# Routing of a mixture of experts in batches of two and four groups, one batch ahead of the shared expert

## The reference

```python
xf = layernorm(x).reshape(-1, 128)
shared = einsum(silu(xf @ sw1) * (xf @ sw3), sw2)      # 256 hidden
logits = xf @ router_w.T + experts_bias                # 8 experts
rw, sel = top_k(logits, 2)
rw = softmax(rw)
moe = sum over the two chosen experts of rw * (silu(xf @ w1[e]) * (xf @ w3[e])) @ w2[e]
x = x + moe + shared
```

## Time and profile before

| | us |
|---|---|
| median of 3 timed runs (lowest, highest) | 1047.42 (1047.19, 1048.82) |
| the profiled execution: its span, which is all that it has as a time of its own | 1165.9 |
| stage of the gates and the mLSTM | 0 to 216 |
| shared part with the routing | 216 to 451.6 |
| routed part | 451.6 to 624 |
| attention | 624 to 1024 |
| per-expert FFN | 1024 to 1166 |

### The profile page before, as it was taken

How to read it: one execution, slowest core, us unless ns; L and a number is a source line. 1 busy time by engine, 2 the same in 40 slices (tenths; PEclk the granted TensorE clock), 3 DMA queues, 4 the chain that set the end, 5 groups by cost and what they waited for, 6 DMA issues and landing times. The chain is left out here.

```text
span 1165.9 us, 24805 instructions
## 1 busy us (share of the span) xinstructions
PE 969.0 (83%) x9121; PEld 680.7 (58%) x9121; DVE 734.8 (63%) x2271; ACT 535.2 (46%) x848; POOL 505.3 (43%) x566
## 2 busy tenths in 40 slices
PE   6819998667787749999994478888888899989998
PEld 1217776444444426666662267777777778856665
DVE  7676999765566545877774555554555556445553
ACT  2457886432333325666665134453444446332221
POOL 4202675676566652555555773344533531011110
PEclk9869998677879768999998578888888989999999
DMA  8554553321222235333332111101110210024331
GB/s 258 192 148 138 159 165 106 128 89 51 57 61 66 61 89 149 109 124 123 119 119 82 46 33 33 29 28 38 44 31 29 83 49 21 21 65 111 93 93 36
DMA packets 84600, 101.29 MB, mean 87 GB/s; under 512 B 36129, under 2 KB 57313, under 8 KB 83713
## 3 DMA queue, kind: packets, MB, share of 16 engines
q1 hardware_dynamic: 73552, 81.61, 23.5%
q0 software_dynamic: 8192, 16.79, 4.7%
q10 hardware_dynamic: 2736, 1.31, 0.4%
HBM read 64.81 MB, written 30.67 MB: 82 GB/s over the span
## 5 line engine op out<-in xcount | busy, mean ns | idle before, releaser
L1728 ACT ACTIVATE split_table<-attn_psT 128x1024 f32<-128x1024 f32 x64 | 65.5, 1023 | 170.0 <-DMA early_ctxT<-in_ctxT 95.9
L1039 POOL TENSOR_TENSOR moe_h_lo<-moe_hid,moe_h_hi 128x512 f16<-128x512 f32 x78 | 90.3, 1158 | 100.2 <-ACT moe_h_hi L1196 95.4
L1619 PE MATMUL attn_psO<-heads_vheads,split_table 128*64 128x18 f32 x2048 | 87.2, 220 | 30.1 <-issue 30.0
L1302 DVE SCALAR_TENSOR_TENSOR moe_hid<-moe_psU,split_to_hidden,moe_act_g 128x512 f32<-128x512 f32 x110 | 81.0, 748 | 36.5 <-ACT moe_act_g L1190 36.4
L1190 ACT ACTIVATE moe_act_g<-moe_psG,split_unscale 128x512 f32<-128x512 f32 x110 | 75.7, 688 | 59.7 <-PE moe_psU L1121 38.6
L1619 PEld LDWEIGHTS attn_psO<-heads_vheads,split_table 128*64 128x64 f32 x2048 | 78.3, 148 | 41.6 <-issue 39.7
L1791 DVE TENSOR_REDUCE split_table<-attn_psN 128x16 f32<-128x1024 f32 x62 | 75.8, 1222 | 22.4 <-DMA early_ctxT<-in_ctxT 9.6
L1815 DVE RECIPROCAL split_table<-attn_psO 128x16 f32<-128x16 f32 x64 | 16.5, 257 | 112.7 <-PE attn_psO L1619 50.8
L1033 POOL DMA_INDIRECT scratch_xs<-cell_xn,res_row x64 | 63.3, 989 | 42.4 <-DVE res_row L1296 25.2
L1196 ACT ACTIVATE moe_h_hi<-moe_hid 128x512 f16<-128x512 f32 x110 | 68.5, 623 | 24.3 <-DVE moe_hid L1302 23.3
L1033 POOL DMA_INDIRECT scratch_xs<-moe_xn,res_row x64 | 62.6, 978 | 37.2 <-DVE res_row L1296 19.4
(11 more groups left out here) (282 smaller groups left out, 2762.9 us busy)
## 6 DMA issues: line engine op xcount, KB each, us to landing
early_ctxT<-in_keys SPq DMA_DIRECT2D x16, 512.0 KB, 3.5
scratch_ys<-cell_h SPq DMA_DIRECT2D x26, 256.0 KB, 2.0
early_ctxT<-in_values SPq DMA_DIRECT2D x8, 544.0 KB, 3.5
mlstm_vals<-in_values SPq DMA_DIRECT2D x8, 544.0 KB, 3.5
res_x<-in_x SPq DMA_DIRECT2D x16, 256.0 KB, 6.2
early_ctxT<-in_ctxT SPq DMA_DIRECT2D x16, 256.0 KB, 6.5
attn_in_ctxT<-attn_in_ctxT SPq DMA_DIRECT2D x64, 64.0 KB
scratch_x<-split_table SPq DMA_DIRECT2D x16, 256.0 KB
```

The costliest lines, as they stand in the source:

```text
L1039: pool.tensor_tensor(h_lo[u % 3][c][:, :], hid[u % 2][c][:, :], h_hi[u % 3][c][:, :], ALU.subtract).then_inc(lo_done[c], 1)
L1302: v.scalar_tensor_tensor(out=hid[u % 2][c][:, :], in0=psU[c][:, :], scalar=sw.to_hidden[:, 0:1], in1=act_g[c][:, :], op0=ALU.mult, op1=ALU ...
L1619: ins = pe.matmul(psO[i % 2][b2 * S:(b2 + 1) * S, at * 2 * VW1:(at + 1) * 2 * VW1], probT[i % 2][:, rr, b2, mp, n * S:(n + 1) * S], vheads ...
L1728: act.activation(probT[i % 2][:, :, :, :, :].rearrange("p r b m q -> p (r b m q)"), psT[:, :], ACT.Exp).then_inc(prob_done, 1)
```

## The change

Routing is done in batches of groups, (0,1), (2,3), (4 to 7), (8 to 11), (12 to 15), one batch ahead of the shared expert. A group that is routed gets transposes of its own (`turn_route`, copied by ACT in `route_out`), apart from those of the shared expert, through the same bank `psT`. In iterations g with g % 4 of 0 or 1 and g < 12 two groups of the next batch are normalised, transposed and routed. For a whole batch there is one pass of logits and choice (`read_logits`, `settle`; maxima and indices still go by tiles), at g % 4 = 2, one `tensor_tensor_scan` for the sums over tiles, two count matmuls, and one `place_`, at g % 4 = 3; the running sum enters as the first element of the scan, so `carry` goes. Batches 0 and 1 are routed ahead of the loop, except for count and placing of batch 1, which come in iteration 0. The normalised groups have eight buffers, four of them views of the weight buffers of the routed part, whose first copies therefore wait for scatters and transposes. The slot map is made at g = 12 instead of after the loop, and the tails are cleared from there; K and V are projected two groups behind, in pairs for the last four, so none is left after the loop.

POOL's order is as before. The core of the diff:

```diff
+BATCHES = ((0, 2), (2, 2), (4, 4), (8, 4), (12, 4))
+BATCH_OF = [k for k, (_, n) in enumerate(BATCHES) for _ in range(n)]
+BATCH_TILES = max(n for _, n in BATCHES) * TILES
...
+        held = [wt[k][:, :, :].rearrange("p w h -> p (w h)").bitcast(F32)[:, 0:GROUP].rearrange("p (t d) -> p t d", t=TILES) for k in range(NW)]
+        xb = [xn[0], xn[1], held[0], held[1], xn[2], xn[3], held[2], held[3]]
...
+        def routed_at(g):
+            first = (g // 4 + 1) * 4 + g % 4 * 2
+            return (first, first + 1) if g % 4 < 2 and first < GROUPS else ()
+
+        def projected_at(g):
+            if g < BEHIND:
+                return ()
+            return (g - BEHIND,) if g < GROUPS - BEHIND else (GROUPS - 4 + 2 * (g - GROUPS + BEHIND), GROUPS - 3 + 2 * (g - GROUPS + BEHIND))
...
-            for g in range(GROUPS - AHEAD):
+            for g in range(GROUPS - LAST_MOVES):
                 move_values(sp, g)
-            sp.wait_ge(tails_done, ONE + 1)
-            for e in range(E0 - ACT_TAILS):
-                clear_tail(sp, e)
+                if g == GROUPS - 6:
+                    sp.wait_ge(tails_done, ONE + 1)
+                    for e in range(E0 - ACT_TAILS):
+                        clear_tail(sp, e)
...
-                pool.wait_ge(placed, ONE + g + 1)
+                pool.wait_ge(placed, ONE + BATCH_OF[g] + 1)
...
+            def turn_route(n):
+                pe.wait_ge(xn_done, ONE + max(n - 1, 0))
+                pe.wait_ge(x_lo_done, ONE + reads["shared"])
+                pe.wait_ge(xnT_done, ONE + n)
                 for t in range(TILES):
-                    ins = pe.matmul(psR[:, t * E0:(t + 1) * E0], xnT[g % 2][:, t * P:(t + 1) * P], router[:, :], start=True, stop=True)
+                    ins = pe.transpose(psT[:, t * P:(t + 1) * P], xb[n % XN][:, t, :], ident[:, :])
+                ins.then_inc(route_turned, 1)
+                reads["routed"] = n + 1
...
+            def count_(k):
+                n = BATCHES[k][1] * TILES
+                pe.wait_ge(either_done, ONE + k + 1)
+                pe.wait_ge(placed, ONE + k)
+                if k == len(BATCHES) - 1:
+                    pe.matmul(psC, every[:, :], sums_of[n][:, :, n], start=True, stop=True)
+                pe.matmul(psK[:, 0:E0 * n], earlier[:, :], chain_of[n][:, :, 1:n + 1], start=True, stop=False)
+                pe.matmul(psK[:, 0:E0 * n], every[:, :], sums_of[n][:, :, 0:n], start=False, stop=True).then_inc(counted, 1)
...
+            turn_route(0)
+            turn_route(1)
+            route(0)
+            route(1)
+            turn_route(2)
+            turn_route(3)
+            route(2)
+            route(3)
+            count_(0)
             turn(0)
...
+                if g == 0:
+                    count_(1)
+                if new:
+                    turn_route(new[0])
+                if g == BEHIND:
                     pe.wait_ge(given.loaded, ONE + 16 * given.count)
-                if g >= AHEAD:
-                    project_k(g - AHEAD)
+                behind = projected_at(g)
...
+                if new:
+                    route(new[0])
+                    turn_route(new[1])
                 if g >= 2:
                     down(g - 2)
-                count_(g)
-                if g >= AHEAD:
-                    project_v(g - AHEAD)
-            total()
-            for g in range(GROUPS - AHEAD, GROUPS - 1):
-                project_k(g)
-                if g == GROUPS - 2:
-                    down(g)
-                project_v(g)
+                if new:
+                    route(new[1])
+                if behind:
+                    project_v(behind[0])
+                if g % 4 == 2 and g < GROUPS - 4:
...
+            def read_logits(k):
+                first, groups = BATCHES[k]
+                n = groups * TILES
+                v.wait_ge(routed, ONE + first + groups)
+                v.tensor_tensor(logits[:, 0:n, :], psR[:, 0:E0 * n].rearrange("p (t e) -> p t e", e=E0),
+                                bias[:, :].unsqueeze(1).to_broadcast([P, n, E0]), ALU.add).then_inc(logits_read, 1)
+                v.wait_ge(logits_read, ONE + k + 1)
+                for t in range(n):
...
+            def settle(k):
+                first, groups = BATCHES[k]
+                n, cols = groups * TILES, slice(first * TILES, (first + groups) * TILES)
+                step(v.tensor_copy(wheref[:, 0:n, :], where[:, 0:n, 0:2]))
+                step(v.tensor_tensor(chosen[:, cols, :, :], wheref[:, 0:n, :].unsqueeze(3).to_broadcast([P, n, 2, E0]),
+                                     iota[:, :].unsqueeze(1).unsqueeze(1).to_broadcast([P, n, 2, E0]), ALU.is_equal))
+                if k:
+                    v.wait_ge(counted, ONE + k)
+                    was = BATCHES[k - 1][1] * TILES
+                    v.tensor_copy(chain_of[n][:, :, 0], sums_of[was][:, :, was])
+                else:
+                    v.memset(chain_of[n][:, :, 0], 0.0)
+                step(v.tensor_tensor(chain_of[n][:, :, 1:n + 1].rearrange("p e t -> p t e"), chosen[:, cols, 0, :], chosen[:, cols, 1, :], ALU.add))
+                v.tensor_tensor_scan(sums[:, 0:E0 * (n + 1)], keeps[n][:, :, :].rearrange("p e t -> p (e t)"), chains[:, 0:E0 * (n + 1)],
+                                     0.0, ALU.mult, ALU.add).then_inc(either_done, 1)
+                v.wait_ge(either_done, ONE + k + 1)
...
+                if j < NW:
+                    n = XN + (2, 3, 6, 7)[j]
+                    v.wait_ge(scattered[n % XN], 16 * 2 * TILES * (GROUPS // XN))
+                    v.wait_ge(turned, ONE + n + 1)
...
+            normalise(2)
+            normalise(3)
             cell.next_statistics(v, GROUPS - 3)
+            v.wait_ge(front.loaded, ONE + 16 * len(front.consts))
+            read_logits(0)
+            settle(0)
+            place_(0)
             low_x(0)
-            v.wait_ge(front.loaded, ONE + 16 * len(front.consts))
-            choose(0)
+            read_logits(1)
+            settle(1)
...
+                for n in routed_at(g):
+                    normalise(n)
                 gated(g, 0)
                 gated(g, 1)
+                if g == 0:
+                    place_(1)
                 if g < 2:
                     cell.next_statistics(v, GROUPS - 2 + g)
-                if g + 2 < GROUPS:
-                    normalise(g + 2)
-                place_(g)
-                ins = carry(g)
-                if g + 1 < GROUPS:
-                    step(ins)
-                    choose(g + 1)
-                else:
-                    ins.then_inc(either_done, 1)
+                if g % 4 == 3 and g < GROUPS - 4:
+                    place_(g // 4 + 2)
+                if g % 4 == 2 and g < GROUPS - 4:
+                    read_logits(g // 4 + 2)
+                    settle(g // 4 + 2)
                 low_part(g)
                 if g >= 2:
                     add(g - 2)
-            map_tiles()
+                if g == GROUPS - 4:
+                    map_tiles()
```

More of the change, by code:

```diff
@@ L941, in phase_moe @@
         hid = [[r.sb(f"hid{u}{c}", [P, GROUP]) for c in range(CH0)] for u in range(2)]
-        past, past_tiles = (hid[0][c][:, 0:SLOT_TILES * E0].rearrange("p (j e) -> p j e", e=E0) for c in range(2))
-        full = past_tiles[:, 0:GROUPS, :].rearrange("p g e -> p e g")
         h_hi = [[r.sb(f"h_hi{u}{c}", [P, GROUP], F16) for c in range(CH0)] for u in range(3)]
@@ L1014, in _ @@
                 load(j)
-            for g in range(GROUPS - AHEAD, GROUPS - 1):
+            for g in range(GROUPS - LAST_MOVES, GROUPS - 1):
                 move_values(sp, g)
@@ L1054, in _ @@
         def _(pe):
+            reads = {"shared": 0, "routed": 0}
             def turn(u):
@@ L1178, in xT_out @@
                 act.wait_ge(turned, ONE + u + 1)
-                if u < GROUPS:
-                    if u >= 2:
-                        act.wait_ge(routed, ONE + u - 1)
-                    act.activation(xnT[u % 2][:, :], psT[:, :], ACT.Copy)
                 if u >= 2:
@@ L1185, in xT_out, with route_out @@
                 act.activation(x_hi[u % 2][:, :], psT[:, :], ACT.Copy, scale=X_SCALE).then_inc(x_hi_done, 1)
+            def route_out(n):
+                act.wait_ge(route_turned, ONE + n + 1)
+                if n >= 2:
+                    act.wait_ge(routed, ONE + n - 1)
+                act.activation(xnT[n % 2][:, :], psT[:, :], ACT.Copy).then_inc(xnT_done, 1)
             def gate(u, c):
@@ L1215, in _ @@
                     high_part(u - 1, 1)
+                if new:
+                    route_out(new[0])
                 gate(u, 1)
                 high_part(u, 0)
-                if u >= AHEAD:
-                    k_out(u - AHEAD)
-            v_out(GROUPS - 1 - AHEAD)
-            high_part(GROUPS - 1, 1)
-            for g in range(GROUPS - AHEAD, GROUPS - 1):
-                k_out(g)
-                v_out(g)
-                if g == GROUPS - AHEAD:
+                if behind:
```

(37 more changed lines are left out.)

129 lines of the change are left out of this document (58 added, 71 removed).

## The result

The changed kernel takes 1073.61 us in the median of four runs (1068.45 to 1086.33), the kernel before 1047.31 in the same comparison. The ratio is 1.0225 with a 95% interval of 1.0183 to 1.0267: 24 us slower, between 19 and 28 (the run at 1086.33, which had the lowest mean clock, is left out of it). The prediction said 1070 and slower.

A forecast was written before the change was run, and what follows sets the result against it. It took POOL's chain of scatters, 10.1 us a group, to bound the shared stage, the other engines' loop close behind. Timed 1047.4 + 10.5 (late startup and loop) + 12 (clock) = 1070 us, range 1036 to 1090.

The forecast's parts named there:

- The reading of the first profile: Shared stage and attention: the profile's waits are not in timed runs; scatters end at 396, routed stage begins about 404.
- The missing 118 us: Profiled span over timed median: 71 us in attention groups under the gathers plus 47 us ahead of the routed stage.
- The 4.87 us between the count and the addition: Group 14, 405.71 to 410.58: could be real PE work recorded too early, since matmul ends in a profile are estimates.
- POOL's second step: Root and scatter(1) wait for statistics(15): scatter(1) at 253 to 257, POOL idle 9 to 13 us more.
- The loop: PE, ACT and DVE in the shared stage: iterations of 12.3, 12.2 and 8.2 us, 143 us from low_x(2).
- The clock: PE idle about 3.2 us in eight iterations drops to half clock: 2.8 us each, 0 to 22, taken as 12.
- One sign of the list: Profile of the changed kernel: granted clock below 0.8 in the shared stage.
- K and V ahead of the routed part: Last four groups' K and V leave the time after the loop: gives 0 to 2 us.
- Eight buffers: Normalised groups, eight buffers instead of four: remove waits not seen in the profile, 0 us.
- The scan: Running sum on DVE: between 0.2 and 0.7 us per batch, 0.3 taken; five make 1 us either way.
- That the stalls are real: Rival, faster: late count releases also in timed runs, POOL's 44.5 us of waiting go; 1002 to 1022; chance 0.20 with milder form.
- POOL bound on both sides: Rival, same: statistics(15) ready before 241, iterations under 10.1 us, scatters end as now, 1047 us; chance 0.07.

The follow-up runs named there:

- the second profile: The kernel before, unchanged, profiled once more: 1047.91 us, span 1046.1.
- the clock held up: Changed kernel with unused matmuls on PE in its idle time ahead of routing transposes and batch counts: 1069.07 us, ratio 1.0192.
- the late root: Changed kernel with POOL's root of the last four groups behind scatter(3) instead of scatter(0): 1071.92 us, ratio 1.0216.
- the run with the early high part: Changed kernel with ACT's second high part made at the end of its own iteration, not behind the next one's first gate: 1061.52 us, ratio 1.0128.
- the kernel with two edits: Changed kernel with ACT's second high part at its own iteration's end and POOL's root behind scatter(3): 1046.57 us, ratio 0.9973.
- the late count: Changed kernel with a batch's count on PE moved from the settling iteration's end to behind up of the next: 1065.72 us, ratio 1.0146.
- the kernel with three edits: Changed kernel with root behind scatter(3), normalisations one iteration early and count behind up of the next iteration: 1062.47 us, ratio 1.0135.

## Why the prediction was right

**The reading of the first profile** held. The missing 118 us belong to that execution: in the second profile the last scatter starts at 393.75 (said: ends at 396), the routed part begins at 405 (said: 404), an attention group takes 16.8 us. The 4.87 us between the count and the addition were no real work of PE recorded too early either: the same addition waits 0.5 us in all in the second profile. Whoever had believed the first profile would have forecast 35 us faster.

**POOL's second step.** Said: statistics(15) done at 250 to 254, scatter(1) at 253 to 257, 9 to 13 us later than before. Measured: 254.5, 258.5 and, since the clean profile before has 241.32 and not 244.74, 17 us later. The cause was right, the size too small, by 4 us at the upper end of what was said: low_x(2) came at 248.86, just behind the span of 244 to 248.

**The loop.** Said at full clock: 12.3, 12.3, 12.2 and 8.2 us, 45.0 for four. Measured with the clock held up: 12.1, 12.1, 12.4 and 8.0, 44.6. From low_x(2) to low_x(15) it said 143 us; with the clock held up it was 146.1, in the changed kernel 155.8. (The parts listed for the settling iteration add up to 11.9 and not to the 12.2 that is written; nothing hangs on it.)

**The clock.** Said: idle times of 3.2 us in eight iterations, 0 to 22 us, 12 taken. Measured: seven gaps of 3.0 to 4.2 us, five of them with half clock, 8 us in twelve iterations. One sign of the list was missed: the granted clock was to be below 0.8 in the stage and was 0.82.

**The sum** put 10.5 and 12 one upon the other, 22.5 us; the timed runs give 24. It is the sum of one path, the loop's, on which the late start and the clock lie one behind the other, and measured by itself (with the late root) that path costs 23 us. Beside it stands POOL's path, whose late second step costs 1.28%, 13 us, by itself (the run with the early high part); the longer one counts. The prediction had both paths at 413 to 417 at full clock, and POOL's last scatter at 405 to 409. In the profile the last scatter starts at 416.55, since the last batch's slots come only at 376.5, and the first up at 430.84. That the number is met so closely is partly luck: the loop started 1 to 5 us later than said and ran 3 us longer, the clock took some 2 us less than the 12, and the profiled execution got back 5 us in the code behind the shared part, which the prediction had put at nothing.

**The terms set to nothing.** K and V ahead of the routed part, 0 to 2 us: nothing in the runs contradicts it, but their new place was not free, since in pairs they lengthen the last two iterations by 5 to 8 us; moved to other iterations they cost as much or more. Eight buffers: the prediction said that the waits they remove are not seen; in the clean profile they are there, 20.8 us. That removing them gives nothing was not tried by itself; it fits that the kernel with two edits, which has the eight buffers, is as long as the kernel before and bound by the same scatters. The scan takes 0.31 us for a batch of two and 0.44 for one of four, near the 0.3 taken. PE's waits for the sums of 16 tiles are there, 4.1 to 4.2 us three times, and the late count took them away by order alone. The Trainium skill ("Perfetto Trace Analysis", Optimizing Scalar/DVE Operations) advises to break up the instructions of an engine that isn't saturated but causes bubbles on others. The trace agrees on the bubbles; breaking up was not tried, and the kernel with two edits keeps three such waits of 4.2 us and is as fast as the kernel before.

**The rivals.** That the stalls are real: refuted. POOL bound on both sides: it is what the kernel with two edits is. What the prediction did not see is how cheap the chain was to break: it took gate, high part, low part, add and low_x as given, and the place of one ACT instruction made the link. The kernel before has that place too; there the wait is 4.1 us in all instead of 86.9.

## What to carry to other kernels

Ahead of reading waits, set the profiled span beside the timed runs. If it is 10% longer, find out which waits make up the difference, or take the profile again, since a change designed on such waits removes what isn't there. When work is moved one batch ahead, look for every in-order engine that now stands at an instruction whose input comes from the next iteration, and for anything that was hidden in front of the bound engine's second step. And where two paths end close together, an edit that is worth nothing alone may be worth its whole size beside the other: try the pair before dropping it.

## What the runs showed of the hardware

One recorded execution can be slow in places: 1165.9 and 1046.1 us for the same kernel, 46 us of the difference up to the first routed up and 74 in the attention, the two parts in which POOL issues indirect DMAs, while the changed kernel, which issues as many and nearly without a pause, was recorded at its timed 1068.45. Whether the recording caused it is not shown.

Idle times of PE of 2 to 4 us were followed by half clock often, but not each time. In the loop of the changed kernel the three of 4.1 to 4.2 us each came with 6.8 us of half clock; of the four of 3.0 to 3.2 us, those that ended at 299.03 and 346.89 came with 3.4 us of it and those that ended at 286.91 and 334.78 with none. In the kernel with three edits, gaps of 2.03 us that ended at 297.6 and 326.4 were followed by full clock and by half clock. In the kernel with the late count, a gap of 3.17 us that ended at 327.67 was followed by half clock up to 340.45, although PE was busy all that time; that iteration took 18.3 us instead of 12.1. Runs of one program differ alongside: those of the changed kernel took 1068.45, 1069.58 and 1077.64 us at mean clocks of 0.926, 0.925 and 0.917. That the clock makes the difference is not shown by itself.

The 5 us that came back behind the shared part stand beside a difference of the clock too. The stretch of 80 us around the start of the attention, first in the kernel before, then in the changed one:

```profile
580.00:660.00 80.00, 44.69 (x422) 34.02 (x423) 43.11 (x132) 28.28 (x38) 51.51 (x56) 0.66 0.16 47
```

```profile
606.00:686.00 80.00, 44.34 (x496) 33.97 (x496) 48.21 (x147) 32.16 (x43) 54.17 (x60) 0.77 0.17 47
```

The granted clock is 0.66 and 0.77, and the rest of the kernel takes 641 and 636 us. Over the profiles of all the kernels here, which share that code, it lies between 636 and 643 us (the first recording of the kernel before left aside), and the two shortest have the least half clock there, 43 us each, the others 49 to 64. What sets it was not tried.
